# Attention scores as float32r products in two row halves, with one bank per unit and a replanned order

## The reference, cut to what matters

```
scores = jnp.einsum("bhqd,bhkd->bhqk", q_full, k_full) * scale
scores = jnp.where(causal[None, None], scores, -jnp.inf)
probs = jax.nn.softmax(scores, axis=-1)
y = jnp.einsum("bhqk,bhkd->bhqd", probs, v)
...
x = x + _layernorm(_L0_attn_ref(_layernorm(x), ...))
x = x + _layernorm(_L0_ffn_ref(_layernorm(x), ...))
x = x + _layernorm(_L1_attn_ref(_layernorm(x), ...))
x = x + _layernorm(_L1_ffn_ref(_layernorm(x), ...))
```

## Time and profile before

| | us |
|---|---|
| median of 3 runs | 1381.56 (1380.0 to 1381.9) |
| the profiled execution | 1380.59 |
| its span in the trace | 1378.8 |
| PE, DVE, ACT, POOL busy | 1221.0, 1060.0, 721.6, 355.3 |
| TensorE's mean granted clock | 0.939 |

### The profile page before, as it was taken

The page is one execution under the profiler, slowest core; times in us unless marked ns, Lnnn a source line. Parts: engine busy times, 40 slices in busy tenths (PEclk is TensorE's granted clock), DMA queues, the critical chain, the costliest instruction groups (busy, mean ns, idle before and its releaser), DMA issues.

```text
span 1378.8 us, 20038 instructions
## 1 busy us (share of the span) xinstructions
PE 1221.0 (89%) x7192; PEld 509.1 (37%) x7192; DVE 1060.0 (77%) x2746; ACT 721.6 (52%) x919; POOL 355.3 (26%) x568
## 2 busy tenths in 40 slices
PE   1757899999999999889978489999999999987996
PEld 1532222333333332556645122233333323244664
DVE  7748898998998973588863578889899889519776
ACT  1324354677676677433433234466666666863332
POOL 6122111113321112243333221112323211124343
PEclk9977898999999999989999679899999999998999
DMA  4156100210210000000016500004004000000000
GB/s 157 45 161 124 39 2 1 43 51 3 46 49 2 1 1 2 0 32 0 2 35 177 142 37 1 2 1 91 4 2 90 4 2 1 1 2 1 1 32 31
DMA packets 27268, 48.80 MB, mean 35 GB/s; under 512 B 6055, under 2 KB 22953, under 8 KB 24097
## 3 DMA queue, kind: packets, MB, share of 16 engines
q1 hardware_dynamic: 21200, 41.95, 12.3%
q0 software_dynamic: 5392, 5.19, 1.2%
q10 hardware_dynamic: 576, 0.39, 0.1%
HBM read 32.41 MB, written 14.68 MB: 34 GB/s over the span
## 4 chain that ended last, share of the span: by engine, by line
PE 70%; DVE 13%; DMA 7%; POOL 3%; issue 3%; ACT 3%; SPq 1%; ACTq 0%; POOLq 0%; DVEq 0%
PE ps L974 68%; DMA k_parts<-parts 3%; DVE m_tile L867 2%; DMA q_stack<-m_rows 2%; DVE ps L869 2%; DMA q_parts<-parts 2%; DVE region_p L752 1%; POOL q_stack L542 1%; DVE region_p L728 1%; DVE stats L715 1%; ACT region_p L657 1%; PE ps L1117 1%; DVE region_p L925 1%; DVE region_p L841 1%; PE ps L969 1%
## 5 line engine op out<-in xcount | busy, mean ns | idle before, releaser
L657 ACT ACTIVATE region_p<-ps 128x1024 f32<-128x1024 f32 (+3 forms) x640 | 541.7, 894 | 327.2 <-PE ps L974 323.3
L867 DVE TENSOR_REDUCE m_tile<-ps 128x1 f32<-128x512 f32 x768 | 501.7, 685 | 68.0 <-PE ps L974 64.5
L974 PE MATMUL ps<-k_stack,q_stack 96*128 96x512 bf16 (+3 forms) x1280 | 394.8, 371 | 29.4 <-DVE rem L769 11.4
L974 PE MATMUL ps<-q_stack,k_stack 99*128 99x512 bf16 (+3 forms) x1280 | 336.3, 358 | 19.2 <-DMA q_stack<-m_rows 16.5
L974 PE MATMUL ps<-region_p,region_vst 128*17 128x512 f32 (+3 forms) x2560 | 295.7, 535 | 4.4 <-POOL region_p L547 4.4
L869 DVE CUSTOM_DVE_ANT_0 ps<-ps,causal 128x128 f32<-128x128 f32 (+3 forms) x512 | 248.4, 498 | 50.7 <-PE ps L974 48.7
L974 PEld LDWEIGHTS ps<-k_stack,q_stack 96*128 96x128 bf16 x1280 | 110.4, 99 | 362.1 <-DVE m_tile L867 157.5
L974 PEld LDWEIGHTS ps<-q_stack,k_stack 99*128 99x128 bf16 x1280 | 115.0, 100 | 157.8 <-ACT region_p L657 44.6
L547 POOL TENSOR_SCALAR_AFFINE_SELECT region_p<-region_p 128x512 f32<-128x512 f32 x128 | 81.4, 637 | 302.7 <-ACT region_p L657 302.1
L974 PE MATMUL ps<-region_a,w_ffn 128*128 128x512 f16 x512 | 123.4, 386 | 6.1 <-DVE region_a L760 5.2
L691 ACT ACTIVATE region_v<-ps,cols 128x512 f32<-128x512 f32 x64 | 44.0, 688 | 127.2 <-PE ps L974 127.1
(11 more groups left out here) (94 smaller groups left out, 938.6 us busy)
## 6 DMA issues: line engine op xcount, KB each, us to landing
k_parts<-parts SPq DMA_DIRECT2D x16, 384.0 KB, 3.1
q_parts<-parts SPq DMA_DIRECT2D x16, 384.0 KB, 3.4
q_stack<-q_parts SPq DMA_DIRECT2D x16, 384.0 KB
k_stack<-k_parts SPq DMA_DIRECT2D x16, 384.0 KB
q_stack<-q_parts SPq DMA_DIRECT2D x16, 256.0 KB
k_stack<-k_parts SPq DMA_DIRECT2D x16, 256.0 KB
X<-in_x SPq DMA_DIRECT2D x4, 512.0 KB, 6.9
q_stack<-q_parts SPq DMA_DIRECT2D x16, 128.0 KB
```

What stands on the lines that cost most here:

```text
L657: nc.scalar.activation(probs[:, o.j % SLOTS, 2 * o.hp:2 * o.hp + 2, o.off:CH], psT[:, o.k % 2, :, o.off:CH], ACT.Exp, scale=SCALE).then_in ...
L867: nc.vector.tensor_reduce(maximum, scores, AX.X, ALU.max).then_inc(s.ring_free, 1)
L974: return pe.matmul(o, a, b, start=first, stop=last)
```

## The change

- **Two parts instead of three.** ACT writes the high part as float32r, DVE the low part at once (`unit_low`); `split_mid` and `split_lo` are gone. Parts are 4 bytes wide and the ring has PB = 4 buffers, of 512 KB a store instead of 384 KB.
- **Row halves.** A head has 48 stack rows (low times high, high times low, high times high); even heads lie in partitions 0 to 63 and odd heads in 64 to 127. S and T are float32r products of 48 and 50 rows in one half of the array's rows.
- **Units.** S alternates between heads of the two halves. T is now one head per item and one bank (`T_HEADS` = 1, 0, 3, 2), with three banks (`TRING`), and one exponential of up to 512 elements per item. The score ring has four banks.
- **The causal mask** is added on PE: two bfloat16 products of `half_eye` and `causal`, 128 and 64 wide, into the diagonal unit's bank. DVE then uses the plain `tensor_reduce` for every S unit.
- **Maxima** have two parts, POOL two operations instead of four.
- **PV in halves**: a tile wider than 256 is two items (256 and 256, or 192 and 192).
- **The plan** has new costs, no priorities (the kind that can start first wins, with the two halves counted apart), no `LEAD`, and another order of steps.

```diff
-PB = 5
-RING = 3
+PB = 4
+RING = 4
+TRING = 3
-STEP_ORDER = [(g, Q) for g in range(NG) for Q in (range(NCH) if g % 2 == 0 else reversed(range(NCH)))]
-LEAD, LEAD_REST = 280, 4
+STEP_ORDER = [(0, 0), (0, 1), (0, 2), (0, 3), (1, 3), (1, 2), (1, 1), (1, 0),
+              (2, 2), (2, 3), (3, 3), (3, 2), (2, 1), (3, 1), (2, 0), (3, 0)]
+T_HEADS = (1, 0, 3, 2)
...
+        def start(kind):
+            free = max(half)
+            if kind == "S":
+                free = max(pe, half[s_units[si][1] % 2])
+            if kind == "T":
+                free = max(pe, half[t_list[ti][3] % 2])
+            return max(free, ready[kind] + LDW)
+
+        kinds = [x for x in ("MT", "YT", "S", "T", "PV") if x in ready]
+        kind = min(kinds, key=start)
...
-        q_stack = sb("q_stack", [P, 2, HALF, HG, TH], BF16)
-        k_stack = sb("k_stack", [P, 2, HALF, HG, TH], BF16)
+        q_stack = sb("q_stack", [P, 2, HALF, HG // 2, TH], F32)
+        k_stack = sb("k_stack", [P, 2, HALF, HG // 2, TH], F32)
...
+                        for e in range(2):
+                            r0 = PAIR * e
...
+                            dmas.append((qs[DH:NSTACK, :], q))
+                            dmas.append((ks[DH:NSTACK, :], k[HI:HI + 1].broadcast_to([2, DH, 2 * TH])))
+                            dmas.append((qs[0:DH, :], q[HI]))
+                            dmas.append((ks[0:DH, :], k[LO]))
...
-                        nc.scalar.activation(probs[:, o.j % SLOTS, 2 * o.hp:2 * o.hp + 2, o.off:CH],
-                                             psT[:, o.k % 2, :, o.off:CH], ACT.Exp, scale=SCALE).then_inc(s.exp_done, 1)
+                        nc.scalar.activation(probs[:, o.j % SLOTS, o.h, o.off:CH], ps[:, o.k % TRING, o.off:CH],
+                                             ACT.Exp, scale=SCALE).then_inc(s.exp_done, 1)
...
-                nc.vector.scalar_tensor_tensor(rem[:, u % 2, :], ps[:, u % 4, :], unit_bias(L, u), parts[:, u % PB, 0, :],
-                                               ALU.add, ALU.subtract).then_inc(p.rem, 1)
+                nc.vector.scalar_tensor_tensor(parts_r[:, u % PB, LO, :], ps[:, u % 4, :], unit_bias(L, u),
+                                               parts[:, u % PB, HI, :], ALU.add, ALU.subtract).then_inc(p.lo, 1)
...
-                        if o.c < o.Q:
-                            nc.vector.tensor_reduce(maximum, scores, AX.X, ALU.max).then_inc(s.ring_free, 1)
-                        else:
-                            nc.vector.tensor_tensor_reduce(scores, scores, causal[:, CH - n:CH], 1.0, MASKED, ALU.add,
-                                                           ALU.max, maximum).then_inc(s.ring_free, 1)
+                        nc.vector.tensor_reduce(m_tile[:, o.n % 2, o.h * TPC + o.r, o.c:o.c + 1], ring_bank(o.ring)[:, 0:n],
+                                                AX.X, ALU.max).then_inc(s.ring_free, 1)
...
+                        ins = mm(bank[:, 0:n], q_r[rows_, o.g % 2, o.Q // CPH, o.h // 2,
+                                                   q_at(o) + o.r * P:q_at(o) + (o.r + 1) * P],
+                                 k_r[rows_, o.g % 2, o.c // CPH, o.h // 2, o.c % CPH * CH:o.c % CPH * CH + n],
+                                 True, not diag)
+                        if diag:
+                            for i in range(2):
+                                ins = mm(bank[:, n - P + PAIR * i:n], half_eye[r0:r0 + PAIR, i, :],
+                                         causal[r0:r0 + PAIR, i, PAIR * i:P], False, i == 1)
...
-                        if o.k >= 2:
-                            pe.wait_ge(s.exp_done, L * T_N + o.k - 1)
-                        for h in range(2):
...
+                        if o.k >= TRING:
+                            pe.wait_ge(s.exp_done, L * T_N + o.k - TRING + 1)
+                        rows_ = slice(PAIR * (o.h % 2), PAIR * (o.h % 2) + KROWS)
...
-                            ins = mm(ps[32 * h:32 * h + VW, PV_BANK, o.off:CH], v_stage[:, o.g % 2, o.kt, h, :],
-                                     probs[:, o.j % SLOTS, h, o.off:CH], o.first, o.last)
+                            ins = mm(ps[32 * h:32 * h + VW, PV_BANK, o.off:o.end], v_stage[:, o.g % 2, o.kt, h, :],
+                                     probs[:, o.j % SLOTS, h, o.off:o.end], o.first, o.last)
```

More of the change, by code:

```diff
@@ L26 @@
 F32 = mybir.dt.float32
+F32R = mybir.dt.float32r
 BF16 = mybir.dt.bfloat16
@@ new lines, in tile_off @@
+    def tile_off(n, kt):
+        Q = steps[n][1]
+        return P * (kt - TPC * Q) if kt >= TPC * Q else 0
+    pv_list = []
+    for n in range(n_steps):
+        for i, kt in enumerate(kts[n]):
+            off = tile_off(n, kt)
+            cuts = [off, (off + CH) // 2, CH] if CH - off > CH // 2 else [off, CH]
+            pv_list += [(n, i, kt, a, b, len(kts[n])) for a, b in zip(cuts, cuts[1:])]
+    pv_tile = []
+    for n, i, kt, a, b, m in pv_list:
+        pv_tile.append(pv_tile[-1] + (a == tile_off(n, kt)) if pv_tile else 0)
@@ L188, in plan_attention @@
+            tile_done = ti % HG == HG - 1
+            last = i == len(kts[n]) - 1 and tile_done
+            order.append(Step("T", n, g, Q, h=h, kt=kt, off=off, k=k, j=ti // HG, first=i < TPC, stop=tile_done, last=last))
+            k += 1
+            if tile_done:
+                exp_end[ti // HG] = act + 0.18
+                if i < TPC:
+                    pool = max(pool, act + 0.15) + 0.65
+                    exp_end[ti // HG] = pool + 0.06
             if last and all(g2 != g for g2, _ in steps[n + 1:]):
-                t_end[g] = pe
+                t_end[g] = t + took
@@ L201, in plan_attention @@
+            pe = t + PV_SWITCH + PV_FULL * (b - a) / CH
+            half = [pe, pe]
+            last = i == m - 1 and b == CH
+            order.append(Step("PV", n, g, Q, kt=kt, off=a, end=b, first=i == 0 and a == 0, last=last, k=pi,
+                              j=pv_tile[pi], sel=sel_used if i < TPC else None))
+            pi += 1
             if last:
-                act = max(act, pe + PE_LAT) + 480
-                v_free = evac[n] = act + SEM_NS
-            pi += 1
+                a0 = max(act, pe + PIPE)
+                act = a0 + 0.49
+                v_free = evac[n] = a0 + 0.66
@@ L542, in _ @@
                             pool.dma_start(dst, src).then_inc(mrows_in[o.n % 2], 16)
-                    if o.kind == "T" and o.first and o.hp == 1:
+                    if o.kind == "T" and o.first and o.stop:
                         pool.wait_ge(s.exp_done, L * T_N + o.k + 1)
```

308 lines of the change are left out of this document (138 added, 170 removed).

## The result

The changed kernel takes **1515.95 us**, the median of four runs from 1487.13 to 1568.63, against 1380.78 for the kernel before, and the prediction had it 97 us faster. As runs of the new versions scatter, every time compared from here on is the median of a kernel's runs within 1.5% of its fastest, which is 1497.7 us for the changed kernel: 117 us slower, a ratio of 1.085 with a 95% interval from 1.072 to 1.098. Its times scatter by 5%, where those of before agree within 0.2%, and they follow the clock: 1487 us at a mean granted clock of 0.847, 1508 at 0.836, 1524 at 0.820, 1569 at 0.789. The profiled execution is the one of 1487.13 us.

What follows compares the result with a forecast made beforehand. PE and DVE were taken as nearly tied: PE 156 + 230 + 11 = 397 us a stage, 405 with 6 for the start and 2 of latency. 1380.59 - 2 x 51 + 2 x 2 = 1282.6, so 1284 us; range 1235 to 1390.

Steps and rivals of the forecast that it cites:

- PV halves, 0.565 us each: PV on PE: 240 items 256 wide at 0.565 us, 156 us a layer with the narrower ones, 18 us more than before.
- Streaming at bf16's rate, halves side by side: S and T on PE: 0.215 us for 512 columns, 232 us a layer, 116 if the row halves run side by side.
- Weights of 0.14 us, one at a time, as the pace: S and T on PE: 1280 weight loads a layer at 0.14 us set the pace, 179 us.
- the prediction's third rival: Weights as dear as float32 products': 0.21 us a load, stage 495 us, 1464 in all, slower from 0.18; chance 0.10.
- The mask, 51 us of PE a layer: Diagonal units on PE: 512 bfloat16 products with 0.1 us of weights each add 51 us a layer.
- The clock: PE in the attention stages: clock read as mostly full in the earlier trace, with no loss put in the sum.
- 2 x 405: The two attention stages, forecast at 405 us each, 51 less than 456.
- The order, 40 us of last part and DVE full to the last S unit: Each stage: DVE busy 350 us until the last S unit, then some 40 us of T and PV, 390 in all.
- PE needs 397 us and no engine gives more than the tie costs: Each stage: PE at 397 us nearly ties with DVE's 390, and nothing is given back for the tie.
- The rival of coupling: Each T waits for ACT, each S for DVE: stage between 397 and 440 us, 1354 in all at 440; chance 0.12.
- Projections, +2 us: Projections: stores, one more unit and the shorter split together add 2 us a layer, bounds -5 and +10.

Runs made afterwards that it cites:

- the patterns: Kernels of products alone, seven patterns and then eight mixes, each begun warm and cold: 0.115 us a float32r product in alternating halves, 0.56 a PV half.
- the old rules: Changed kernel with the old step order, whole PV tiles, S, T and PV ranked as before, 38 us for a stack load: 1446.2 us.

## Why the prediction was wrong

- *PV halves, 0.565 us each:* right. 0.56 in the patterns. That a half also brings another change to row halves and back was not in the sum, beyond PV's own 0.14. 131 more changes a layer at 0.20 are 26 us.
- *Streaming at bf16's rate, halves side by side:* right, 0.115 us a product by itself.
- *Weights of 0.14 us, one at a time, as the pace:* wrong in size and in kind. A load takes 184 ns at full clock, 0.18 us, which by the prediction's third rival is where slower begins. But it is hidden, in alternating halves (0.115 us a product) and in one half alone (0.227). The time came out slower, as the rival said, and not by the rival's mechanism. Part 3 of "TensorE: Matmul & The Clock Gate" in the Trainium skill has a load overlap only work of other row groups; the bf16 rows of before disagree, and so do both patterns. By the rule, as an estimate, one half alone would take 0.184 + 0.215 = 0.40 us a product and two halves 0.20.
- *The mask, 51 us of PE a layer:* far too much, some 13 us for both layers, with overlapping runs.
- *The clock:* **the step that failed.** Every price in "PE has 397 us" is one at full clock; the prediction took the clock from the earlier trace rows as mostly full, put its loss at nothing, and never asked whether the new products keep it so. In the first stage, 108 to 260 us, the mean is 0.56 and was 0.83; the second starts with 120 us at 0.50. The last part of the second stage is 73.3 us instead of the 53.2 it takes at full clock. An estimate of the starts: were DVE as busy in them as before (95.7 of 113 us from 105 on, 108.7 of 122 from 812 on, and 0.91 in the 24 us at 235 and 948), its 79.6, 82.5, 17.0 and 17.3 us of work would take some 59 us less than they did. With the 20 of the last part that is 80 of the 208 us by which the two stages exceed 2 x 405. With the operands undone the clock is 0.94, and 47 us come back under the old rules but 28 in the change's own order; how much of these is the clock isn't shown, since bursts bought 31 us in one order and none in the other.
- *The order, 40 us of last part and DVE full to the last S unit:* **failed too**, and by itself: with bf16 operands and a clock of 0.94 the new order and its halves cost 70 us. The last part takes 53.2 at full clock: two T products and a PV half take 1.08 us where the sum had 0.53 + 2 x 0.16 = 0.85, and 0.98 even alone, with the change that T in ones and twos between PV halves pays each time. (Of its 93 T items 48 are narrower, not 32; the 36 us for ACT are those of 48.) And waits for a stack load, 15.2 us in the first stage and 16.1 in the second, in which PE stands, were left out of the sum altogether.
- *PE needs 397 us and no engine gives more than the tie costs:* wrong. Weights one at a time and the mask gave 230 us for 1280 products, 0.180 each; it is 0.195 at nearly full clock in the middle of the version with the old rules, hardly below bf16's 0.200. The rival of coupling named this (a wait holds back the other's weights), at 440 us a stage; the stages are 493.5 and 524.9.
- *Projections, +2 us:* the first stage begins 2.8 us earlier instead; from the end of the first to the second it is 213.3 us, 2.5 more than before, as put.

The range ended at 1390 because every rival above it was priced by one load or one rate. None had the clock in it, and together they had 0.16. That some rivals said slower is luck, as none of their mechanisms came true as priced.

## What to carry to other kernels

Before operands are packed into parts of the array, count how often the order changes the row arrangement, and price a change by a small kernel: here 0.1 to 0.2 us each, more than a product. Ask of every stretch with waits whether its mix brings the clock back by itself; a busy share of ten tenths says nothing of it, so read PEclk beside it and time the same piece at both levels. And price a product in the mix and order in which it will run, not alone: 0.10 us (at the widths of the kernel) became 0.195.

## What was not expected of the hardware

- A mix of products can hold either clock level: five float32r products in halves and a PV half ran at 1.00 for its whole length behind a warm-up and at 0.50 for its whole length behind a pause, with PE 10.00 of 10 us busy in both.
- The first of the bursts of 40 bf16 products (6.96 us) brought it from 0.50 to 1.00, and the eight together made the whole kernel 31 us faster, while bursts in the kernel before cost 5.1 us each.
- Two small products in a half of the rows between products of 96 rows cost some 0.2 us a pair, 106 us in all; as one product of 128 rows they cost nearly nothing.
- The last 20 us of a group's load of the stacks ran at a DMA share of 0.13, that of two engines of 16, and 50 GB/s, so that a load that was planned at 20 us took 37. The kernel before has such a stretch too (0.13 and 51 GB/s from 948 to 972 us), but there nothing waited for it:

```profile
384.00:400.00 16.00, 15.87 (x162) 8.05 (x160) 14.84 (x29) 12.40 (x30) 4.21 (x6) 1.00 0.85 136
400.00:420.00 20.00, 6.81 (x62) 2.45 (x54) 2.21 (x5) 6.18 (x12) 2.59 (x6) 0.72 0.13 50
```
